# Part of the dt*u*B products made on ScalarE and TensorE in a one-core Mamba block, with more of the products with C on GpSimd

## The reference, cut to what matters

```python
dA  = exp(A[None, :, None, :] * dt[:, :, :, None])
dBu = dt[:, :, :, None] * Bm[:, None, :, :] * hs[:, :, :, None]
def step(h, inp):
    dA_t, dBu_t, C_t = inp
    h = dA_t * h + dBu_t
    y = einsum('bdn,bn->bd', h, C_t)
    return (h, y)
y = (y + hs * D) * silu(gate);  out = einsum('bdl,hd->blh', y, Wout)
```

## Time and profile before

| | us |
|---|---|
| median of 3 runs | 1198.71 (1197.83 to 1200.13) |
| profiled execution, its own time | 1195.93 |
| its span, first to last instruction | 1194.1 |
| busy: DVE, POOL, PE, ACT | 1070.6, 987.8, 939.8, 786.1 |
| DVE busy share in block B | about 96% |
| mean granted TensorE clock | 0.906 |

### The profile page before, as it was taken

How to read it: one execution, slowest core, us unless ns; L and a number is a source line. 1 busy time by engine, 2 the same in 40 slices (tenths; PEclk the granted TensorE clock), 3 DMA queues, 4 the chain that set the end, 5 groups by cost and what they waited for, 6 DMA issues and landing times.

```text
span 1194.1 us, 17013 instructions
## 1 busy us (share of the span) xinstructions
PE 939.8 (79%) x4294; PEld 580.9 (49%) x4304; DVE 1070.6 (90%) x1205; ACT 786.1 (66%) x1117; POOL 987.8 (83%) x783
## 2 busy tenths in 40 slices
PE   4979889666777797877686979786879788777888
PEld 3646556234444454544444545444545444444554
DVE  7867878579999999999999999999999999999994
ACT  4888877656777655767675557676746567777551
POOL 5342534499999999999798999998989999999992
PEclk9999999868878899988988998888979899989999
DMA  8566758871111218332112183221202921212100
GB/s 282 205 245 220 276 194 303 335 282 46 56 50 35 80 61 285 126 111 71 55 34 74 44 322 110 82 71 56 80 27 92 321 95 61 69 44 71 37 1 36
DMA packets 53187, 150.53 MB, mean 126 GB/s; under 512 B 5728, under 2 KB 14048, under 8 KB 50016
## 3 DMA queue, kind: packets, MB, share of 16 engines
q1 hardware_dynamic: 53088, 149.41, 35.9%
HBM read 111.37 MB, written 38.01 MB: 125 GB/s over the span
## 4 chain that ended last, share of the span: by engine, by line
POOL 56%; issue 15%; DVE 4%; PE 2%; ACT 1%; POOLq 1%; DVEq 0%
POOL dbu L928 43%; POOL hp L936 13%; DVE gate_bf L997 1%; DVE hp L982 1%; DVE da L982 1%; PE mm L1025 1%; DVE prod L951 1%; PE da L1025 1%; POOLq L927 0%; PE yT L1103 0%; POOLq L933 0%; ACT gate_bf L867 0%; ACT da L887 0%; ACT L868 0%; ACT L867 0%
## 5 line engine op out<-in xcount | busy, mean ns | idle before, releaser
L887 ACT ACTIVATE da<-unit,neg_a 128x512 f32<-128x512 f32 x512 | 341.6, 686 | 306.9 <-DVE prod L951 296.7
L928 POOL TENSOR_TENSOR dbu<-unit,b_head 128x512 f32<-128x512 f32 x384 | 501.3, 1338 | 11.3 <-issue 5.8
L982 DVE TENSOR_TENSOR_SCAN da<-da,dbu 128x512 f32<-128x512 f32 x320 | 383.1, 1218 | 10.8 <-POOL dbu L928 7.8
L1103 PE MATMUL yT<-ident,prod 128*128 128x128 f32 x1280 | 222.2, 302 | 186.0 <-DVE prod L951 184.7
L1103 PEld LDWEIGHTS yT<-ident,prod 128*128 128x128 f32 x1280 | 158.1, 152 | 312.8 <-DVE prod L951 283.8
L982 DVE TENSOR_TENSOR_SCAN hp<-da,dbu 128x512 f32<-128x512 f32 x192 | 231.8, 1207 | 30.3 <-ACT da L887 16.7
L936 POOL TENSOR_TENSOR hp<-hp,c_head 128x512 f32<-128x512 f32 x160 | 205.3, 1283 | 35.6 <-DVE hp L982 35.3
L928 POOL TENSOR_TENSOR dbu<-unit,b_all 128x512 f32<-128x512 f32 x128 | 160.6, 1282 | 0.0
L1061 PE MATMUL mm<-xn_b,w_sb 128*128 128x512 fp8e4 x512 | 145.2, 425 | 6.2 <-ACT gate_bf L895 5.9
L951 DVE TENSOR_TENSOR prod<-da,c_head 128x512 f32<-128x512 f32 x224 | 149.3, 667 | 0.0
L1103 PE MATMUL yT<-ident,hp 128*128 128x128 f32 x768 | 129.3, 296 | 0.0
(11 more groups left out here) (107 smaller groups left out, 1303.0 us busy)
## 6 DMA issues: line engine op xcount, KB each, us to landing
unit<-unit_d SPq DMA_DIRECT2D x32, 768.0 KB, 4.3
unit_d<-dt_du SPq DMA_DIRECT2D x32, 512.0 KB, 2.7
wf<-in_wffn SPq DMA_DIRECT2D x12, 1024.0 KB, 5.9
c_head<-bc_d SPq DMA_DIRECT2D x24, 512.0 KB, 5.7
b_head<-bc_d SPq DMA_DIRECT2D x18, 512.0 KB, 5.5
unit_d<-hsd SPq DMA_DIRECT2D x32, 256.0 KB, 4.3
w_sb<-w_d SPq DMA_DIRECT2D x64, 128.0 KB, 3.4
wgate<-in_win_gate SPq DMA_DIRECT2D x32, 256.0 KB, 2.6
```

The source lines that it names most:

```text
L887: nc.scalar.activation(da[n % SLOTS][:, :], unit[:, k % 2, 0, :], ACT.Exp, scale=neg_a[:, k, n:n + 1]).then_inc(da_ready, 1)
L928: nc.gpsimd.tensor_tensor(dbu[:, n % DBUS, :], unit[:, k % 2, 1, :], b_all[n // NS][:, n % NS, :], ALU.mult).then_inc(dbu_ready, 1)
L982: nc.vector.tensor_tensor_scan(state, da[n % SLOTS][:, :], dbu[:, n % DBUS, :], 0.0, ALU.mult, ALU.add).then_inc(scanned, 1)
L1103: ins = nc.tensor.matmul(yT[k % 2][:, t * P:(t + 1) * P], product[:, t * P:(t + 1) * P], ident[:, :], start=False, stop=last, is_transpose ...
```

## The change

Each unit now has three sets of states, which differ by unit (`POOLED[k]`, `BY_SCALE[k]`; the rest of each follows by `others`). `Ring` replaces the old arithmetic for the slot and the count of a state in a set.

- For the states in `BY_SCALE` (5 in units 0, 6 and 7, 4 in unit 5, 3 in units 1 to 4) POOL makes no du*B. du is turned once per unit to steps on partitions (piece `u_T` on PE, into a bank `mm`; ACT copies it to `u_T`). There B_n is one scalar per partition, and ACT makes du*B by four 128x128 copies with a scale operand into `scaled` (2 buffers), at its step n-2. PE turns them back by four transposes into PSUM bank `da[n % 4]` (`turn_scaled`), at its position n-4, behind that position's adds and ahead of its other pieces. ACT writes the decay of such a state to `decay` in SBUF. The scan reads decay from SBUF and du*B from PSUM.
- POOL takes 8 products with C (units 0, 6, 7) or 9 (units 1 to 5) in place of 6.
- The buffers for dbu fall from 8 to 5 and those for `prod` from 5 to 4.
- Block A turns the rows of B by four small transposes per batch (`bT_all`).

```diff
-DBUS = 8
-POOLED = (0, 2, 5, 7, 10, 12)
-PRODS = 5
+DBUS, PRODS, HPS, DECAYS, SCALED = 5, 4, 6, 2, 2
+POOL_LAG, PE_LAG, Z_AHEAD = 3, 4, 2
+LIGHT, HEAVY = (0, 2, 3, 5, 7, 8, 10, 12), (0, 1, 3, 4, 6, 7, 9, 10, 12)
+POOLED = (LIGHT, HEAVY, HEAVY, HEAVY, HEAVY, HEAVY, LIGHT, LIGHT)
+FEW, MANY = (5, 9, 13), (4, 6, 9, 11, 14)
+BY_SCALE = (MANY, FEW, FEW, FEW, FEW, (5, 8, 11, 14), MANY, MANY)
+U_T, U_T_AFTER = (4, 5, 5, 5, 12, 6, 5, 5), (0, 0, 0, 0, 0, 0, 0, 0)
+U_T_COPIED = {(0, 8): 0, (1, 9): 1, (2, 9): 2, (3, 9): 3, (5, 1): 4, (5, 10): 5, (6, 9): 6, (7, 9): 7}
...
+    pieces[U_T[k]].insert(U_T_AFTER[k], ("u_T", 0, 0))
...
+            def scale_u(b, k, n, opening):
+
+                act.wait_ge(u_T_ready, b * KU + k + 1)
+                act.wait_ge(bT_ready, b + 1)
+                act.wait_ge(*slot_left(SCALE, dbu_mm, b, k, n))
+                for t in range(LT):
+                    ins = nc.scalar.activation(scaled[:, SCALE.slot(k, n), t * P:(t + 1) * P], u_T[:, k % 2, t * P:(t + 1) * P], ACT.Copy,
+                                               scale=bT[:, t, n:n + 1])
+                ins.then_inc(scaled_ready, 1)
...
+                    if (k, n) in U_T_COPIED:
+                        made = U_T_COPIED[k, n]
+                        act.wait_ge(u_T_mm, b * KU + made + 2)
+                        nc.scalar.activation(u_T[:, (made + 1) % 2, :], mm[plan[(made, "u_T", 0)][0]][:, :],
+                                             ACT.Copy).then_inc(u_T_ready, 1)
+                    if n + Z_AHEAD in BY_SCALE[k]:
+                        scale_u(b, k, n + Z_AHEAD, opening)
+                    target = da[n % SLOTS][:, :]
+                    if n in BY_SCALE[k]:
+                        target = decay[:, DECAY.slot(k, n), :]
...
+            def turn_u(bank, slot):
+                for t in range(LT):
+                    ins = nc.tensor.transpose(bank[:, t * P:(t + 1) * P], unit[:, slot, 1, t * P:(t + 1) * P], ident[:, :])
+                ins.then_inc(u_T_mm, 1)
+
+            def turn_scaled(b, k, n):
+
+                pe.wait_ge(scaled_ready, SCALE.count(b, k, n))
+                pe.wait_ge(*state_left(b, k, n - SLOTS))
+                for t in range(LT):
+                    ins = nc.tensor.transpose(da[n % SLOTS][:, t * P:(t + 1) * P], scaled[:, SCALE.slot(k, n), t * P:(t + 1) * P],
+                                              ident[:, :])
+                ins.then_inc(dbu_mm, 1)
...
+                if name == "u_T":
+
+                    bank = take_bank(b, k, (name, h), opening)
+                    if k < KU - 1:
+                        pe.wait_ge(unit_loaded[(k + 1) % 2], unit_loads(b, k + 1))
```

More of the change, by code:

```diff
@@ L48, with others, __init__, slot @@
 SWITCH, GATED, GELU = 6, 7, 2
-DBUS = 8
-POOLED = (0, 2, 5, 7, 10, 12)
[L51 to L54, removed]
-PRODS = 5
-ADDED = {n: [m for m in POOLED if min(m + PE_LAG, N - 1) == n] for n in range(N)}
+DBUS, PRODS, HPS, DECAYS, SCALED = 5, 4, 6, 2, 2
[4 more added lines that the diff above has]
+BY_SCALE = (MANY, FEW, FEW, FEW, FEW, (5, 8, 11, 14), MANY, MANY)
+def others(states):
+    return tuple(tuple(n for n in range(N) if n not in states[k]) for k in range(KU))
+class Ring:
+    def __init__(self, states, size):
+        self.states, self.size = states, size
+        self.order = [(k, n) for k in range(KU) for n in states[k]]
+        self.total = len(self.order)
+    def slot(self, k, n):
+        return self.order.index((k, n)) % self.size
+    def count(self, b, k, n):
+        return b * self.total + self.order.index((k, n)) + 1
+    def until(self, b, k, n=0):
+        return b * self.total + sum(at < (k, n) for at in self.order)
+    def before(self, k, n):
+        i = self.order.index((k, n))
+        if i >= self.size:
+            return self.order[i - self.size], False
+        return [at for at in self.order if self.slot(*at) == self.slot(k, n)][-1], True
+OWN, BY_POOL = others(POOLED), others(BY_SCALE)
+PROD, HP, DBU, SCALE = Ring(OWN, PRODS), Ring(POOLED, HPS), Ring(BY_POOL, DBUS), Ring(BY_SCALE, SCALED)
+DECAY = Ring(BY_SCALE, DECAYS)
+ADDED = [{n: [m for m in POOLED[k] if min(m + PE_LAG, N - 1) == n] for n in range(N)} for k in range(KU)]
 BANKS = 2
@@ L668, in block_b @@
         y_t = sb("y_t", [P, L])
+        bT = sb("bT", [P, LT, N])
+        u_T = sb("u_T", [P, 2, L])
+        scaled = sb("scaled", [P, SCALED, L])
+        decay = sb("decay", [P, DECAYS, L])
         da = [ps(f"da{i}", [P, L]) for i in range(SLOTS)]
@@ L928, in body @@
-                    nc.gpsimd.tensor_tensor(dbu[:, n % DBUS, :], unit[:, k % 2, 1, :], b_all[n // NS][:, n % NS, :], ALU.mult).then_inc(dbu_ready, 1)
+                    if n in BY_POOL[k]:
+                        if k == 0 and (n % NS == 0 or n - 1 not in BY_POOL[k]):
+                            if n >= G_AHEAD * NS:
+                                pool.wait_ge(b_loaded[n // NS], b * 16 + 16)
+                            elif not opening:
+                                pool.wait_ge(b_loaded[n // NS], b * 16)
+                            elif n == 0:
+                                pool.wait_ge(b_head_loaded, 16 * (B - 1))
+                        if not (opening and DBU.before(k, n)[1]):
+                            pool.wait_ge(*scanned_before(DBU, b, k, n))
+                        nc.gpsimd.tensor_tensor(dbu[:, DBU.slot(k, n), :], unit[:, k % 2, 1, :], b_all[n // NS][:, n % NS, :],
+                                                ALU.mult).then_inc(dbu_ready, 1)
@@ L1050, in beside @@
                 if name == "out_b" and opening:
+                    return
+                if name == "u_T":
+                    bank = take_bank(b, k, (name, h), opening)
+                    if k < KU - 1:
+                        pe.wait_ge(unit_loaded[(k + 1) % 2], unit_loads(b, k + 1))
+                    elif not (isinstance(b, int) and b == B - 1):
+                        pe.wait_ge(unit_loaded[0], unit_loads(b + 1, 0))
+                    turn_u(bank, (k + 1) % 2)
                     return
```

157 lines of the change are left out of this document (96 added, 61 removed).

## The result

The changed kernel takes 1231.04 us (median; 1229.89 to 1233.43), the kernel before 1198.27 (1196.67 to 1200.13) beside it. The ratio is 1.0275, with a 95% interval of 1.0251 to 1.0298: slower, by 33 us. The prediction said 1226 and slower. The profiled execution has a span of 1229.2 us against 1194.1, 35.1 more.

A forecast was written before the change was run, and what follows sets the result against it. DVE and POOL were taken to share the limit. Units 1 to 7 gave +12.0 us, unit 0 +13.8, block A and the first `u_T` +1.5: +27 on 1195.93, 1223, or 1226 as median; range 1205 to 1245.

The forecast's parts named there:

- Unit 5 to 6 and 6 to 7: State 4's turn at position 0 of units 6 and 7, behind the output group and opening: +4.1 and +1.6 us a batch.
- the rest of unit 7: Unit 7 from scan 4 on: DVE sets it instead of POOL, 18.3 us against 21.0, so -2.7 us a batch.
- the wait for ScalarE behind the silu block: Units 0, 6 and 7: fewer products cover the block and state 9's copies follow; 0.7 us each, up to 2 in unit 0.
- Unit 0: `u_T` at position 3 waits for unit 1's tile: 33.3 against 28.2 us, +5.1 in three batches; -1.5 in the first.
- Units 1 to 5 at zero: Held gelu products lengthen some units by 1.8 us, others shorten by 1.6: taken as zero, bounds -8 and +9 a batch.
- The price of a scaled copy: On ACT, a 128x128 copy with scale: 376 ns, from 295 unscaled plus 81; about 1.2 us for a state's copies.
- The wait of scan 3 behind the gelu block: State 5's copies stand between ACT's exps of states 2 and 3, so DVE waits 0.7 us more.
- Scans with decay in SBUF and du\*B in PSUM: On DVE, swapping the memories of a scan's two inputs leaves its time the same: 1.13 us apart, 1.22 long.
- Busy times: DVE busy should fall by about 40 us and POOL by about 50 while the span grows.
- PE is early enough: Rival, chance 0.24: state 4's turn (units 6, 7) and unit 1's tile (unit 0) come in time; faster, 1159 us.
- the product is always held: Rival, chance 0.12: POOL always holds DVE's gelu product in units 1 to 5; +7 us a batch, 1254 us.
- the clock rival: Rival, chance 0.08: a ninth of PE's work in units 6, 7 and 0 at half clock; +8 us a batch, 1258.

The follow-up runs named there:

- three mends: Changed kernel with `u_T` of unit 1 turned later in unit 0, state 4 not scaled in units 6 and 7, state 5 instead of 6 on GpSimd: 1187.16 us, 0.9882.

## Why the prediction was right, and where its sizes were off

- *Unit 5 to 6 and 6 to 7.* Predicted +4.1 and +1.6, less 2.7 for the rest of unit 7: 3.0 a batch. Measured 3.9, and 4.1 and 4.4 in the first and the last batch. PE's opening ended 8.26 us after the first scan (676.76 less 668.50), 7.83 before and 9.13 predicted; scan 4 waited 3.15 us, where 4.1 was said, so PE was less behind than the three groups of transposes added to it. What was missing from the sum is the wait for ScalarE behind the silu block, priced at 0.7 among what the change adds and then left out: it is 1.25 us in unit 6 (686.91). In unit 7 the wait was 3.20 where 2.8 was said, and from scan 4 to the end the unit took 18.28 (724.34 less 706.06), predicted 18.3. Exchanging state 4 for a later one gave 19 us back, so this cause is shown.
- *Unit 0.* Predicted 33.3 us long, measured 34.0 to 34.6; in the first batch 24.6, 2.4 shorter, predicted 1.5. TensorE waited for the load as said, 7.96 us. The load was there 13.7 us after the unit's start (738.07 less 724.34), not 12.5, and from there to the last add it took 19.7 (757.75 less 738.07), not 20.8, so two errors of size offset each other. And the prediction took all of the loss for this wait, which was wrong as a mechanism: without the wait unit 0 is still 32.9 us long. That its 33.3 came so near is in part luck. The bank that `u_T` takes from the ffn groups, and ScalarE's order, were not in the reckoning.
- *Units 1 to 5 at zero.* Measured +2.7 us in the whole run, between units shorter by 4 and longer by 3.4. The zero was a choice between bounds of -8 and +9 a batch, not a sum, so that it held is partly luck too. Unit 2 of the middle batches has 31.4 and 31.3 where 31.9 was said for a held product. DVE's 1.76 us a unit did not come through: GpSimd still has 22 tiles, and the gelu product waits for its pause. This was the step where a gain was expected from the diff and none came. One detail was wrong: the clip was counted at 1.58 us; it took 0.94, with GpSimd pausing by then, and the gelu product took the difference, and more.
- *The price of a scaled copy.* 376 ns estimated, 388 measured, and 1.17 us from one group of four to the next instruction (1.2 said). The wait of scan 3 behind the gelu block that was to come of it, 0.7, is 0.54 to 0.63 us in fifteen of the twenty units and nothing in five. The group of copies:

```profile
L934 ACT ACTIVATE scaled<-u_T,bT 128x128 f32<-128x128 f32 x496 | 156.8, 388 | 0.0
```

- *Scans with decay in SBUF and du\*B in PSUM* take the same 1.22.
- *Busy times.* DVE -37.5 (-40 said), POOL -59 (-50 said).
- *The rivals.* That PE is early enough fell with the 3.15 and 3.20. That the product is always held fell in the middle batches' units 1 (26.3 us, product 0.95), though the mean over the twenty is now 3.8. The granted clock is 0.94 in unit 6 (1.00 before) and 1.00 in unit 7, which holds five turns and `u_T`; 0.85 in unit 0, where it was 0.82; in the mean 0.913 against 0.906. Nothing is seen there of the clock rival's 32 us.
- *The sum.* 27 us predicted and 35.1 measured in the profiled executions: 4.2 of the rest lie in units 6 and 7 with the end of the program, 1.2 in unit 0 and 2.7 in units 1 to 5; ahead of block B it was 1.3 where 1.5 was said.

What stays open: what else sets unit 0, and when VectorE is let in between GpSimd's tiles. Taking `u_T` out of the two ffn banks, or placing the scaled copies behind the ffn copies, wasn't tried.

## What to carry to other kernels

When work is moved to idle engines, ask for each moved piece by when it is wanted and what stands ahead of it in its new queue: here 19 of the 33 us hung on which of 16 states was scaled first in two units of eight. When two engines that exclude each other share the limit, the place where one of them pauses matters as much as its count of tiles: exchanging one state for another was worth 16 us, and with 20 products moved back to DVE the kernel was 21 us faster. Try mends together, for single ones showed 2 + 19 + 16 us and the three 47.

## What the runs showed that had not been expected

- A bf16 product of two SBUF tiles on VectorE was held by GpSimd's back-to-back tiles for up to 8.97 us (with 24 tiles a unit). In the changed kernel it took up to 5.63 us with all columns and still up to 5.11 with 8.
- The reverse case exists too, a product of 1536 columns in 1.22 us, and GpSimd's two tiles beside it longer by 0.7 us together.
- Taking products off GpSimd made VectorE less busy: 1008.8 us with 20 more of them, against 1014.2 with the same three mends.
